# Exponential of the norms written to PSUM, a buffer of its own for the low part of the tokens, and new orders on all engines

## What is computed

```python
def l2norm(t):
    return t / jnp.maximum(jnp.linalg.norm(t, axis=-1, keepdims=True), 1e-12)

def attn_layer(x, Wqkv, qs, ksc, Wo):
    q, k, v = jnp.split(x @ Wqkv, 3, -1)          # 16 heads of 64
    q = l2norm(q) * qs
    k = l2norm(k) * ksc
    q = q * cos * scale + rotate_half(q) * sin * scale
    k = k * cos / scale + rotate_half(k) * sin / scale
    out = local_attention(q, k, v)                # softmax in windows of 32, own and previous window
    return out @ Wo

def ffn_layer(x, g, bln, W1, b1, W2, b2):
    xn = (x - mu) / jnp.sqrt(var + 1e-05) * g + bln
    a, gate = jnp.split(xn @ W1 + b1, 2, -1)
    return a * gelu(gate) @ W2 + b2

for i in range(6):
    x = attn_layer(shift_tokens(x), ...) + x
    x = ffn_layer(shift_tokens(x), ...) + x
```

## Time and profile before

| | |
|---|---|
| median of three runs | 3580.86 us (3575.13 to 3580.91) |
| profiled execution | 3578.89 us, its span 3577.1 us |
| PE busy | 3154.9 us, 88% |
| DVE busy | 3164.0 us, 88% |
| ACT busy | 2295.4 us, 64% |
| POOL busy | 1896.4 us, 53% |
| granted TensorE clock, mean | 0.964 of full |

### The profile page before, as it was taken

One profiled execution on the slowest core, in us unless ns is written; L12 is line 12 of the kernel. 1 busy time (PEld: TensorE's weight loads), 2 busy tenths in 40 slices (PEclk: granted clock), 3 DMA queues, 4 the chain that ended last, 5 costly groups with the idle time before them and its releaser, 6 DMA issues. The chain is left out here.

```text
span 3577.1 us, 72114 instructions
## 1 busy us (share of the span) xinstructions
PE 3154.9 (88%) x25560; PEld 1980.7 (55%) x25560; DVE 3164.0 (88%) x2723; ACT 2295.4 (64%) x3693; POOL 1896.4 (53%) x823
## 2 busy tenths in 40 slices
PE   6768999999999999999956799999999999999996
PEld 3445655555556555555533555555555555555553
DVE  4458999999999999999924899999999999999995
ACT  1146776776777767767712577777776767777773
POOL 4435655556555655556500656555656565556561
PEclk8679999999999999999978999999999999999998
DMA  5434454454454454454411445445445445445442
GB/s 186 150 110 97 97 142 104 99 140 108 97 141 103 103 136 103 109 133 105 99 40 67 92 102 132 114 99 135 113 101 130 114 100 134 111 101 136 114 98 68
DMA packets 273779, 399.12 MB, mean 112 GB/s; under 512 B 75837, under 2 KB 104249, under 8 KB 273721
## 3 DMA queue, kind: packets, MB, share of 16 engines
q1 hardware_dynamic: 273720, 398.48, 45.4%
HBM read 66.34 MB, written 19.92 MB: 24 GB/s over the span
## 5 line engine op out<-in xcount | busy, mean ns | idle before, releaser
L935 POOL TENSOR_TENSOR f_ab<-f_w,f_rn 128x1024 f32<-128x1024 f32 x192 | 644.7, 3358 | 1013.2 <-DVE f_rn L963 1013.2
L953 DVE TENSOR_TENSOR f_w<-f_ab,f_tan 128x1024 f32<-128x1024 f32 x384 | 730.2, 1940 | 49.3 <-ACT f_ab L810 44.8
L930 POOL TENSOR_TENSOR f_u<-f_u 128x512 f32<-128x512 f32 x384 | 662.1, 1742 | 46.5 <-ACT f_u L809 46.5
L932 POOL TENSOR_TENSOR f_w<-f_w,f_ab 128x1024 f32<-128x1024 f32 x192 | 505.2, 2631 | 285.6 <-DVE f_w L953 285.6
L809 ACT ACTIVATE f_u<-ps 128x512 f32<-128x512 f32 x768 | 459.8, 599 | 215.4 <-PE ps L623 190.4
L679 PE MATMUL ps<-f_tb,f_v 128*64 128x160 f32 (+1 forms) x6144 | 456.4, 303 | 133.6 <-DMA f_tb<-f_pt 97.8
L810 ACT ACTIVATE f_ab<-ps,f_pa 128x512 f32<-128x512 f32 x768 | 533.2, 694 | 0.0
L679 PEld LDWEIGHTS ps<-f_tb,f_v 128*64 128x64 f32 x6144 | 409.7, 141 | 214.8 <-issue 134.7
L621 PE MATMUL ps<-f_xh,f_wh 128*128 128x512 f32 x768 | 403.1, 525 | 29.9 <-DMA f_pa<-pa 17.5
L658 PEld LDWEIGHTS ps<-f_kb,f_qb 128*32 128x32 f32 x12288 | 327.6, 111 | 156.6 <-issue 136.9
L658 PE MATMUL ps<-f_kb,f_qb 128*32 128x128 f32 x12288 | 380.2, 276 | 24.6 <-DMA f_qb<-f_ab 24.6
(11 more groups left out here) (169 smaller groups left out, 5023.5 us busy)
## 6 DMA issues: line engine op xcount, KB each, us to landing
f_kb<-f_ab SPq DMA_DIRECT2D x1536, 64.0 KB, 2.0
f_qb<-f_ab SPq DMA_DIRECT2D x768, 128.0 KB, 2.4
f_tb<-f_pt SPq DMA_DIRECT2D x1344, 64.0 KB, 2.0
f_wh<-split_w SPq DMA_DIRECT2D x48, 384.0 KB, 4.3
f_wl<-split_w SPq DMA_DIRECT2D x48, 384.0 KB, 4.4
a_w_raw<-wqkv SPq DMA_DIRECT2D x24, 384.0 KB, 3.9
split_w<-a_w_hi SPq DMA_DIRECT2D x24, 384.0 KB, 2.3
split_w<-a_w_lo SPq DMA_DIRECT2D x24, 384.0 KB, 2.8
```

What stands on the lines that cost most here:

```text
L930: nc.gpsimd.tensor_tensor(u[:, 2 * i + 1, :], u[:, 2 * i, :], u[:, 2 * i + 1, :], ALU.add).then_inc(sq_sum[i].sem, 1)
L932: nc.gpsimd.tensor_tensor(w[:, 0:2, :], w[:, 0:2, :], ab[:, k % 2, 0:2, :], ALU.add).then_inc(q_sum.sem, 1)
L935: nc.gpsimd.tensor_tensor(ab[:, k % 2, 0:2, :], w[:, 0:2, :], rn[:, 0:1, :].broadcast_to([128, 2, N]), ALU.mult).then_inc(rope_q.sem, 1)
L953: nc.vector.tensor_tensor(w[:, a:4:2, :], ab[:, k % 2, 1 - a:4:2, :], tan2[:, a:a + 1, :].broadcast_to([128, 2, N]), ALU.mult).then_inc(tu ...
```

## The change

The logarithm and the exponential of the norms stay in PSUM banks 3 and 4; the gain instruction of DVE reads them there and writes `rn`. ACT no longer waits for quad g - 1's `rope_q` and `rope_k` ahead of them, and PE's `values` waits for `gain` where it waited for `n_log`:

```diff
-                            act.wait_ge(rope_q.sem, now.count(rope_q, g - 1))
-                            act.wait_ge(rope_k.sem, now.count(rope_k, g - 1))
                             act.wait_ge(n_ready.sem, now.count(n_ready, g))
                             for i in range(2):
-                                nc.scalar.activation(rn[:, i, :], ps[:, NO[i], :], ACT.Ln, scale=2.0 ** PRE).then_inc(n_log.sem, 1)
+                                nc.scalar.activation(ps[:, NO[i], :], ps[:, NO[i], :], ACT.Ln, scale=2.0 ** PRE).then_inc(n_log.sem, 1)
-                            nc.scalar.activation(rn[:, :, :], rn[:, :, :], ACT.Exp, scale=-0.5).then_inc(n_inv.sem, 1)
+                            nc.scalar.activation(ps[:, NO[0]:NO[1] + 1, :], ps[:, NO[0]:NO[1] + 1, :], ACT.Exp, scale=-0.5).then_inc(n_inv.sem, 1)
...
-                            nc.vector.scalar_tensor_tensor(out=rn[:, :, :], in0=rn[:, :, :], scalar=NORM_FLOOR_INV / 2 ** (PRE // 2), in1=cos2[:, :, :],
+                            nc.vector.scalar_tensor_tensor(out=rn[:, :, :], in0=ps[:, NO[0]:NO[1] + 1, :], scalar=NORM_FLOOR_INV / 2 ** (PRE // 2), in1=cos2[:, :, :],
...
+                            pe.wait_ge(gain.sem, now.count(gain, at))
                             for pair in range(2):
-                                pe.wait_ge(n_log.sem, now.count(n_log, 2 * at + pair))
```

The low part gets the buffer `xl`, so `next_tokens` waits for `x_lo` of the step before and not for the last `v_ready`, and stands right behind `queries(0)` in SP's list. ACT's `xh` waits for that `v_ready` instead. On SP `load_qkv` of the first two quads moves from behind `next_tokens` to between `keys(3)` and `queries(3)`:

```diff
-                xl = xs[:, :].bitcast(F32R)
+                xl = t("xl", [C, N], F32R)
...
-                            sp.wait_ge(v_ready.sem, now.count(v_ready, 2 * TILES - 1))
+                            sp.wait_ge(x_lo.sem, now.count(x_lo, -1))
...
                             queries(0)
+                            next_tokens()
...
-                            next_tokens()
-                            if next_layer is not None:
-
-                                load_qkv(layer_rows, range(2))
...
                             keys(3)
+                            if next_layer is not None:
+
+
+                                sp.wait_ge(v_ready.sem, now.count(v_ready, 2 * TILES - 1))
+                                load_qkv(layer_rows, range(2))
                             queries(3)
```

```diff
-                        for k in range(QUADS if cur else 0):
...
+                        if cur:
+                            add_squares(0)
+                            add_queries(0)
+                            normalise_queries(0)
+                            add_squares(1)
+                            add_squares(2)
+                            add_queries(1)
+                            normalise_queries(1)
+                            add_queries(2)
+                            normalise_queries(2)
+                            add_queries(3)
+                            add_squares(3)
+                            normalise_queries(3)
```

More of the change, by code:

```diff
@@ L621, in project @@
                                 nc.tensor.matmul(bank("qk", g, i), wh[:, g, i, :], xh[:, :], start=True, stop=False)
-                                nc.tensor.matmul(bank("qk", g, i), wh[:, g, i, :], xl, start=False, stop=False)
+                                nc.tensor.matmul(bank("qk", g, i), wh[:, g, i, :], xl[:, :], start=False, stop=False)
                                 nc.tensor.matmul(bank("qk", g, i), wl[:, g, i, :], xh[:, :], start=False, stop=True).then_inc(qk_ready.sem, 1)
@@ L718, in second @@
                             last.then_inc(F["w2"].sem, 1)
+                        if prev:
+                            mask_scores(-1)
                         if cur:
@@ L724, in step @@
                             pe.wait_ge(x_lo.sem, now.count(x_lo, -1))
-                            project(0, (0, 1))
-                        if prev:
-                            values(-3)
-                        if cur:
-                            project(0, (2, 3))
+                            project(0, range(4))
                             if not prev:
@@ L733, in step @@
                         if prev:
-                            mask_scores(-1)
+                            values(-3)
                             project_out(0)
@@ L750, in step @@
                             norms(1)
-                            project(2, (0, 1))
+                            mask_scores(0)
+                            project(2, range(4))
+                            scores(0)
+                            project_v(1, range(2))
                         if prev:
                             project_out(2)
+                            values(-1)
                         if cur:
-                            scores(0)
-                            project(2, (2, 3))
-                            project_v(1, range(2))
+                            mask_scores(1)
                         if prev:
-                            values(-1)
                             project_out(3)
@@ L766, in step @@
                         if cur:
-                            mask_scores(1)
                             scores(1)
@@ L785, in step @@
                             scores(2)
+                            norms(3)
                         if prev:
@@ L901, in step @@
                         if cur:
-                            evacuate_v(1, range(2, 3))
+                            exponentials(1)
                         if prev:
@@ L905, in step @@
                         if cur:
-                            exponentials(1)
-                            evacuate_v(1, range(3, TILES))
-                            evacuate_out(0, (0,))
+                            evacuate_v(1, range(2, TILES))
                         if prev:
@@ L912, in step @@
                             act.wait_ge(xs_done.sem, now.count(xs_done))
+                            act.wait_ge(v_ready.sem, now.count(v_ready, 2 * TILES - 1))
                             nc.scalar.activation(xh[:, :], xs[:, :], ACT.Copy).then_inc(x_hi.sem, 1)
+                            evacuate_out(0, (0,))
                             inverse_norms(3)
@@ L1005, in step @@
                             less_maximum(-1)
+                            sums(-1)
                         if cur:
@@ L1020, in step @@
                         if cur:
-                            turn_weights(0)
+                            turn(2)
                             add_keys(2)
@@ L1040, in step @@
                             gated(0)
-                        if cur:
-                            dve.wait_ge(x_hi.sem, now.count(x_hi))
-                            nc.vector.tensor_tensor(xl, xs[:, :], xh[:, :].bitcast(F32), ALU.subtract).then_inc(x_lo.sem, 1)
-                        if prev:
                             gated(1)
@@ L1047, in step @@
                         if cur:
+                            dve.wait_ge(x_hi.sem, now.count(x_hi))
+                            nc.vector.tensor_tensor(xl[:, :], xs[:, :], xh[:, :].bitcast(F32), ALU.subtract).then_inc(x_lo.sem, 1)
+                            add_keys(3)
                             less_maximum(2)
                             normalise_keys(3)
+                            sums(2)
                         if prev:
```

38 lines of the change are left out of this document (14 added, 24 removed).

## The result

| | median of five runs, us | range |
|---|---|---|
| before | 3578.64 | 3572.76 to 3580.91 |
| after | 3595.09 | 3594.54 to 3602.07 |

The ratio is 1.0053, with a 95% interval of 1.0038 to 1.0068: the change made the kernel slower by 0.5%, 16 us. The forecast was 3495, faster. The profiled execution took 3594.74 us with a span of 3593.0 us, and its mean granted TensorE clock is 0.942, where it was 0.964 before.

A forecast was written before the change was run, and what follows sets the result against it. DVE was taken to bound the regular step, busy 63.10 of 64.82 us. From the profiled 3578.9 us, -134 for regular steps and +49 for layer changes gave 3494, as a median 3495; range 3400 to 3562.

The forecast's parts named there:

- load_qkv: SP's queue at layer changes: first six weight DMAs moved behind keys(3) cost 7 us each, 49 us in all.
- The queue's own share of the layer change: SP walked in issue order: scores(-1) 2.7 us later, queries(0) another 2.9, load_ff about 1.4 in the step after.
- The regular step: One step of the transformer stages falls from 64.82 to 61.9 us, 134 us over 46 steps.
- DVE's own work: DVE in a regular step: 63.1 us less 8.4 of contention with POOL leaves 54.7 us.
- Contention between DVE and POOL: Collisions left in a regular step under the new orders: 2.0 us at four places instead of 8.4.
- The waits: New DVE waits in a regular step: 1.1 and 1.9 at exponentials, 1.5, 0.3 and 0.45 elsewhere; 5.25 us.
- The operand in PSUM: DVE's gain instruction reading the exponential from PSUM: no price against SBUF, within 0.02 us per instruction, and no stretching.
- The port: DVE instructions with two SBUF inputs stretch beside POOL's, as if one engine stood still; 8.4 us a step.
- The own buffer and the early tokens: Buffer xl and earlier next_tokens: ACT's removed wait gives 0, SP's moved issues are free in a regular step.
- D: Rival: slower, DVE and POOL contention goes on; at 6 us a step 66, total 3684; chance 0.10.
- B: Rival: PE becomes the bound, 60.7 us a step, about 3410 us, 3390 to 3465; chance 0.25.
- E: Rival: within 0.2%, gain and loads cancel or the orders don't do what they say; chance 0.05.

The follow-up runs named there:

- experiment 1: Changed kernel with the first six load_qkv DMAs put back behind queries(2): 3503.88 us against 3573.46 for the kernel before, ratio 0.98.
- experiment 2: Kernel before with only the first six load_qkv DMAs moved between keys(3) and queries(3): 3708.81 us against 3573.46, ratio 1.0381.
- experiment 4: Kernel before, old orders, with only the exponential kept in PSUM: 3527.36 us against 3573.46, ratio 0.9869.
- experiment 5: experiment 1 with the exponential of the norms back in SBUF, new orders kept: 3572.52 us against 3573.11 for the kernel before, ratio 0.9993.
- experiment 6: experiment 1 with POOL's old order, each quad's squares, addition and product together: 3546.74 us, ratio 0.9926.
- experiment 10: Kernel before with only the own buffer xl and next_tokens behind queries(0): 3567.41 us against 3577.89, ratio 0.9973.
- experiment 7: experiment 1 with load_ff one step later, behind weights(-1) of a layer's second step: 3492.28 us, ratio 0.9773.
- experiment 8: Changed kernel with all twelve weight DMAs behind queries(2) and load_ff one step later, behind weights(-1): 3466.11 us, ratio 0.9704.
- experiment 9: Changed kernel with all twelve weight DMAs behind queries(2) and SP's loops written out: 3461.43 us against 3577.89 for the kernel before, ratio 0.9677.
- experiment 11: experiment 9 with the second six weight DMAs behind weights(1) and load_ff one step later: 3405.54 us against 3579.12 for the kernel before, ratio 0.9511.

## Why the prediction was wrong, point by point

**load_qkv, the step that failed.** The prediction said of it that it costs 7 us a layer change, 49 us in all, "between bounds of 0 and 10 x 7.5"; the layer change is at 18.7. I walked SP's queue behind the six DMAs and asked who comes late there (queries(3), weights(2), queries(0)). I didn't ask the other half of the question: who waits for the moved DMAs' own data, and when. That is project(0) of the very next step, a first instruction on PE's list, and the earlier trace rows together with the walk's own numbers had all that was needed: keys(3) are issued from 2 to 7, the loads from 7 to 10, quad 0's are the first three, done at 8.5, the data 2 to 2.5 later, and PE wants them at 0. That is some 11 us, and 11.57 was measured. I had even taken the old place as one "with nothing urgent behind", which is true of the queue and false of the data. Experiments 1 and 2 show the cause in both directions. The upper bound of 7.5 was no bound, since it held one mechanism only.

**The queue's own share of the layer change** was too low too. The walk had 2.7 us for scores(-1), 2.9 for the second six and 1.4 for load_ff. The first doesn't show in the changed kernel, since scores(-1) start at 755.26, long after the wait for the weights. The other two make 4.3; experiment 1, where the moved six are out of the way, has 9.6 us a layer change: 3.9 to 5.5 in the first step and 3.3 to 7.0 in the second. For the second I had no term for the pause at the jump back, 3.0 to 3.6 us in the first stage. It was there in the profile before (3.4 to 3.9 us behind load_ff in the first stage), and I hadn't looked for it. In the changed kernel the second steps of the first stage have 6.9 to 7.7 us at the four changes with that pause and 3.4 at the fifth, where the loop ends and the gap is 0.42.

**The regular step: the right total, from wrong pieces.** Forecast 61.9, measured 61.61 and 61.63, and every kernel with the new orders and the PSUM operand has 61.6. The pieces, in the step shown:

- DVE's own work: forecast 54.7. It is 57.77 - 4.1 = 53.7. The 8.4 us of contention in the kernel before were 1.0 too few: the step of the earlier trace rows has some 9.4. An undisturbed pair of turns takes 2.35 us and not 2 x 1.22, and L958, which also has two SBUF inputs, was left out (mean 1.30, 1.18 to 1.23 undisturbed).
- Contention between DVE and POOL: forecast 2.0 at four named places. They measure 0.87 (L975 of quad 1), 0.57 (L996 of quad 0), 0.36 (L975 of quad 2) and 0.41 (L996 of quad 1), 2.2 in all. But three others, which I had not seen, add 1.9: 0.93 at turn(0), 0.76 at the product of quad 0, 0.20 at L996 of the step before. POOL's timeline has their reason: its product of quad 3 begins late and runs over into the next step, so the squares of quad 0 fall on turn(0), and POOL's addition on the product.

```profile
874.31 3.36 POOL L929 TENSOR_TENSOR f_ab<-f_w,f_rn 128x1024 f32<-128x1024 f32 x1 [6.34 <-DVE f_rn L971]
877.63 3.48 POOL L920 TENSOR_TENSOR f_u<-f_u 128x512 f32<-128x512 f32 x2
883.41 3.42 POOL L924 TENSOR_TENSOR f_w<-f_w,f_ab 128x1024 f32<-128x1024 f32 x1 [2.29 <-DVE f_w L961]
```

- The waits: forecast 5.25. The two at the exponentials are there with 1.33 and 1.12 (1.9 and 1.1 expected), ACT's deviation with 0.26 (0.45). The 1.5 for n_inv(0) and the 0.3 for scores(-1) don't show: turn(0) takes 3.28 us in place of 2.35 and so ends nearer to when ACT is through. The contention that I missed lies where I had put a wait. Sum 2.7.
- Gaps between DVE's instructions that no releaser ends: 61.61 - 57.77 - 2.71 = 1.1 us, left out of my sum. The step of before had as much, 64.82 - 63.10 - 0.48 = 1.2.

Own work 1.0 below the forecast, contention 2.1 above, waits 2.5 below and 1.1 forgotten: that the total was within 0.3 is partly luck. It is partly not, since a wait and a contention in the same place stand for one another, and the loop that I had walked through PE and ACT would set the step whichever of them fills it; that last part is argued, no run tests it.

**The operand in PSUM.** Predicted at 1.22 us everywhere: 192 instructions between 1212 and 1226 ns. Neither my bound of 0.02 us nor the estimate of 65 ns that the Trainium skill's page (VectorE: DVE Perf Modes, the section on the TRN2 errata) would make of it shows in any row. Neither loss happened.

**The port.** The prediction took the stretch for one engine standing still for the other. The runs bear it out: the form with a PSUM input never stretches (experiments 1 and 4), the same one from SBUF does again in the new orders (experiment 5, 2.09 us), and POOL's order alone moves 43 us (experiment 6). By the Trainium skill (SBUF — State Buffer, the section "Who interferes with whom") a DVE instruction with two SBUF inputs contends with a GpSimd one that reads SBUF, and the lock on the ports that they share is exclusive; these runs agree, and add that what one DVE instruction is spared the next one with two SBUF inputs may pay: 0.6 of 1.8 us in experiment 4.

**The own buffer and the early tokens**, priced at 0. In a regular step that holds; at the layer changes of the kernel before it gives 1.5 us each (experiment 10).

**values behind gain** instead of n_log, priced at 0: in the kernel after, no group of PE's values has a wait for L971 worth more than 1.2 us in the whole execution. The forecast of 0 was right.

**The rivals.** D had the right sign by the wrong mechanism: it needed contention above 3.8 us a step in steps that would then be longer, and there are 4.1, yet the step is shorter, since less of it is waiting (2.7 for 5.25) and DVE's own work is 53.7. B did not come (60.7 a step), as PE does wait, 1.4 us in the step shown. E is 9 us off. The case that occurred, a layer change at 18.7 us, was in none of them, and the range ended at 3562. With the layer change right, the same sum gives 3578.9 - 134 + 166 = 3611, against 3594.7 of the profiled execution.

**What stays open.** That the pause on SP comes from fetching instructions is likely, not shown: it stands at jumps back of the loop over the layers, moved with the jump (experiments 7 and 8), and went when there was none (experiment 9, which also made constants of SP's registers). Why the same jumps leave only 0.85 us in the second stage of the kernels whose loop ends behind load_ff isn't known. How much of experiment 11's last 56 us belongs to the second six and how much to load_ff was not taken apart. How much of the 18.7 us is standing still and how much is running slower was read for one first step (11.57 and 1.4), not for the rest; over the whole execution the clock is at 0.942 with these waits and back at 0.964 in experiment 11, where they are gone.

## What to carry to other kernels

A DMA that is moved in a queue has two bills: those behind it come later, and its own readers get their data later. For the second, write down beside the new issue time the time at which the first reader wants it, in the next iteration too; a prefetch whose reader is the first instruction of the next step must be issued in this one, never behind something that waits for this step's end. Read rare steps (a layer change, 10 of 48) with the same care as regular ones: 17 us at ten of them ate 3.2 us at forty-six. Where DVE and POOL share work, count the DVE instructions with two SBUF inputs beside POOL's running time; reading one input from PSUM took an instruction off that list here at no price that a row shows.

## What the runs showed of the hardware that I had not expected

- The jump back of a loop over a long body can cost SP's queue about 3 us without an issue. In the kernel after the last load's issue ends at 821.34 + 0.35 = 821.69 and the next one begins at 825.00, 3.3 us; the four jumps back of the first stage have 3.3 to 3.8. In experiment 8 it is 857.09 - 854.30 = 2.8 us, at all eight jumps back of both stages; written out, 0.09 us (799.29 - 799.20, experiment 9). But the same four jumps in the second stage of the kernel after (and of the kernel before) take only 0.84 to 0.87 us, and where the loop ends it is 0.42. The rows of a jump in the first stage of the kernel after, and of one in the second:

```profile
821.34 0.35 SPq L489 DMA_DIRECT2D f_pf<-pf  x1
825.00 4.97 SPq L516 DMA_DIRECT2D f_kb<-f_ab  x8
...
2305.89 0.35 SPq L489 DMA_DIRECT2D f_pf<-pf  x1
2307.11 4.96 SPq L516 DMA_DIRECT2D f_kb<-f_ab  x8
```

  The Trainium skill (Runtime: NRT & Kernel Launch, the section on instruction fetch) says that a taken branch to a page that isn't loaded has to fetch it by DMA before execution goes on. That would fit: one packet of an instruction queue lies in each of the four long pauses of the kernel after and in each of the eight of experiment 8, and none in the short ones of the second stage. No run here separates it from other costs of a jump, and why the second stage is spared the fetch is open.
- In these runs DVE's fp32 forms of 1024 columns take the same time from PSUM as from SBUF undisturbed, and never stretch from PSUM: 1212 to 1226 ns in 192 instructions.
- Freed from contention, DVE doesn't get all of it back: in experiment 4 0.6 of 1.8 us went to the next instruction with two SBUF inputs, and in the kernel after the mean of L975 is 1.61 us, where before it was 1.23.
